# Releasing the row gathers by buffer and indices alone in a graph-convolution kernel

## The reference

```python
msg = relu(x[src] + edge_attr)                      # one message per edge
agg = segment_sum(msg, dst, num_segments=12500)
h = (1.0 + eps[0]) * x + agg
out = layernorm(x + h @ W.T + b)                    # over the 32 features
```

## Time and profile before

| what | value |
|---|---|
| time of the profiled execution | 2931.13 us |
| its span, first to last instruction | 2929.0 us (2.1 us lie around it) |
| median of the three timed runs | 2930.49 us |
| TensorE (PE) busy | 2382.3 us, 81% of the span |
| DVE / ACT / POOL busy | 1812.9 / 1635.8 / 1434.8 us (62 / 56 / 49%) |
| DMA, mean | 81 GB/s |
| mean granted clock of TensorE | 0.909 |

### The profile page before, as it was taken

The page is one execution under the profiler, slowest core; times in us unless marked ns, Lnnn a source line. Parts: engine busy times, 40 slices in busy tenths (PEclk is TensorE's granted clock), DMA queues, the critical chain, the costliest instruction groups (busy, mean ns, idle before and its releaser), DMA issues. The chain is left out here.

```text
span 2929.0 us, 110879 instructions
## 1 busy us (share of the span) xinstructions
PE 2382.3 (81%) x49112; PEld 1842.9 (63%) x35800; DVE 1812.9 (62%) x4504; ACT 1635.8 (56%) x1720; POOL 1434.8 (49%) x1467
## 2 busy tenths in 40 slices
PE   4788888888888888788888888888887878888788
PEld 2566666666666666666666666666666666666664
DVE  5766666666666666665665656666666566565665
ACT  4655555555555555555555555555555555555554
POOL 4454545544545454455455445445555545545541
PEclk9988999989989899989999999898899999898988
DMA  5333333333333333333333333333333333333332
GB/s 123 68 86 79 81 81 79 86 76 78 86 77 81 83 76 83 81 79 85 78 78 86 79 76 86 76 84 81 78 86 79 79 82 79 86 79 76 86 79 50
DMA packets 244832, 236.54 MB, mean 81 GB/s; under 512 B 107748, under 2 KB 190750, under 8 KB 244805
## 3 DMA queue, kind: packets, MB, share of 16 engines
q1 hardware_dynamic: 198053, 212.15, 31.1%
q0 software_dynamic: 46752, 24.03, 5.8%
HBM read 233.21 MB, written 2.78 MB: 81 GB/s over the span
## 5 line engine op out<-in xcount | busy, mean ns | idle before, releaser
L550 POOL DMA_INDIRECT rows_all<-in_x,index x1461 | 1434.3, 982 | 1442.6 <-PE l L1162 611.9
L1144 PE MATMUL found<-table,oh 128*128 128x128 bf16 x13312 | 1288.3, 227 | 12.7 <-issue 11.9
L1184 PE MATMUL found<-table,oh 128*128 128x128 bf16 x6656 | 1271.7, 233 | 21.2 <-issue 12.8
L1184 PEld LDWEIGHTS found<-table,oh 128*128 128x128 bf16 x6656 | 928.3, 139 | 335.8 <-issue 122.5
L1162 PE MATMUL l<-xparts,oh 128*57 128x96 bf16 x19968 | 717.0, 225 | 434.3 <-issue 434.2
L1162 PEld LDWEIGHTS l<-xparts,oh 128*57 128x57 bf16 x19968 | 590.8, 121 | 560.0 <-issue 559.2
L798 DVE COPY_PREDICATED rows_all<-mask,found 128x256 f32<-128x256 uint16 x832 | 370.3, 445 | 657.5 <-PE found L1144 507.0
L971 ACT CAST table<-l 128x768 bf16<-128x768 f32 x416 | 330.3, 795 | 661.7 <-PE l L1162 632.4
L780 DVE TENSOR_SCALAR oh<-keys,lanes 128x1024 bf16<-128x1024 f16 x624 | 295.6, 489 | 190.9 <-PE found L1144 139.8
L1015 ACT ACTIVATE oh<-keys,minus_lanes 128x1024 bf16<-128x1024 f16 x208 | 238.9, 1148 | 264.6 <-PE found L1144 222.1
L996 ACT ACTIVATE oh<-slots,minus_lanes 128x1824 bf16<-128x1824 f16 x208 | 375.2, 1804 | 6.8 <-DMA slots<-slot_dram 6.8
(11 more groups left out here) (127 smaller groups left out, 1031.0 us busy)
## 6 DMA issues: line engine op xcount, KB each, us to landing
slots<-slot_dram SPq DMA_DIRECT2D x208, 456.0 KB
keys<-key_dram SPq DMA_DIRECT2D x208, 256.0 KB
msg<-in_edge SPq DMA_DIRECT2D x208, 128.0 KB
rows_all<-in_x,index POOLq DMA_INDIRECT x1461
msg<-in_edge SPq DMA_DIRECT2D x208, 112.0 KB
index<-in_src SPq DMA_DIRECT2D x208, 3.5 KB
key_dram<-key SPq DMA_DIRECT2D x208, 2.0 KB
slot_dram<-slot_row SPq DMA_DIRECT2D x208, 3.6 KB
```

Of the source, the lines that this page charges most:

```text
L550: pool.indirect_dma_start(to, None, x, bass.IndirectOffsetOnAxis(indices[:, j:j + 1], 0)).then_inc(done, 16)
L1144: return nc.tensor.add_instruction(mybir.InstMatmult(name=nc.get_next_instruction_name(), engine=mybir.EngineType.PE, ldweights=False, ins ...
L1184: last = nc.tensor.matmul(to, key_marks(b)[:, :, t], part, start=begin, stop=end, skip_group_check=True)
```

## The change

The three turns become one. The gathers of a batch wait only until the batch that had the buffer has been added up and until the indices are there; the waits for `l1_ready` and `blocks_looked` are gone, and so are two of the three raises of `gathers_started`. The program order of everything else is as it was.

```diff
-    TURNS = [(0, 3), (3, 5), (5, POOLED)]
...
-                    for k, (j0, j1) in enumerate(TURNS):
-                        if k == 0:
-                            if not free:
-
-                                pool.wait_ge(sums_ready, b - RING + 1)
-
-                                pool.wait_ge(l1_ready, (b - RING + 2) * KEYS)
-                            pool.wait_ge(index_loaded[slot], use * 16 + 16)
-                        elif not free:
-
-                            pool.wait_ge(blocks_looked, (b - RING + 1) * KEYS + k * KEYS // 2)
-                        pool.sem_inc(gathers_started, 1)
-                        for j in range(j0, min(j1, SHORT) if isinstance(b, int) and b == 0 else j1):
-                            gather_tile(rows[slot][:, j * D:(j + 1) * D], index[slot], j, rows_gathered[slot])
+                    if not free:
+                        pool.wait_ge(sums_ready, b - RING + 1)
+                    pool.wait_ge(index_loaded[slot], use * 16 + 16)
+                    pool.sem_inc(gathers_started, 1)
+                    for j in range(SHORT if isinstance(b, int) and b == 0 else POOLED):
+                        gather_tile(rows[slot][:, j * D:(j + 1) * D], index[slot], j, rows_gathered[slot])
```

## The result

The changed kernel takes 3633.74 us (median of 4 runs, 3616.01 to 3640.16) where the kernel before takes 2929.66 us beside it: ratio 1.2394, 95% interval 1.2358 to 1.2430. The forecast was 3144 us with a range up to 3400: the sign was right, but the rise was put at 213 us and came out at 704. A row of work takes (3585.4 - 33.9) / 207 = 17.16 us where it took 13.77.

What follows compares the result with a forecast made beforehand. TensorE, busy 81%, bounds the kernel, losing 2.1 us per row to pauses from gathers. A row of 14.4 us plus 0.4 for the clock, 14.8 against 13.77, over 207 rows adds 213 to 2931: 3144 us, range 2850 to 3400.

Steps and rivals of the forecast that it cites:

- The pauses are the gathers': Bucket stage: TensorE's instructions trickle from 0.9 us after a gather's issue starts until 1.0 us after it ends.
- The rival "same": Pauses come from the loop's jump back ahead of the bucket stage, so moving gathers changes nothing: 2930 us, chance 0.07.
- The Trainium skill's rule on taken branches: A taken branch to outside the fetched window stalls; the 2.1 us would stand every loop turn, time staying 2930 us.
- Where the gathers go: Seven gathers in one 8.7 us burst, released by `add_rows`, from +4.7 to +13.4 us after the bucket stage's start.
- What comes back: Bucket stage without pauses: at most 2.1 us per row regained by TensorE.
- The pieces before: Kernel before: gathers of 3, 2 and 2, the first two pieces hidden in the table stage, the last pausing the bucket stage.
- the reserve: About 70 instructions already handed to TensorE, on which it runs at full pace before pausing; refilled between the gathers' turns.
- The trickle's price: TensorE's time per instruction while gathers hold it up: range 94 to 476 ns, 247 ns taken, giving 14.4 us per row.
- For each I follow two rows: Row lengths worked out per trickle price; at 247 ns the first row ends at 13.75 us, the second at 15.1, mean 14.4.
- the clock's 0.4: Longer starved pieces lower TensorE's granted clock: one more 1.3 us loss in three rows, 0.4 us per row.
- Faster: Rival: the burst leaves the bucket stage and the table stage carries it; 13.2 us per row, 2813 us, chance 0.22.
- Much slower: Rival: long-burst trickle with a clock drop, or rows alternating in length at 156 ns; 16.1 us per row, 3413 us, chance 0.13.

Runs made afterwards that it cites:

- experiment 8: Kernel before with its gathers in other pieces; on starved chips 4 and 3 0.9935, that a quarter early 1.0071, turns 1 and 2 a block early 1.0397.
- Experiment 4: Changed kernel with `count_ranks` moved behind the last table block: 3538.55 us, ratio 1.2346 to the kernel before, on a starved chip.

## Why the prediction had the sign and not the size

**The pauses are the gathers': right.** One gather instead of seven, or plain DMAs, takes a row from 17.16 us to about 10 on starved chips. The rival "same", that the loop's jump makes the pauses, falls with that: the jump is there in all of them. The Trainium skill's rule on taken branches ("Runtime: NRT & Kernel Launch", section Instruction fetch mechanics), weighed in the prediction, is not what stalls here: with the same jump the bucket stage's line sat idle for 16.9 us over the span with plain DMAs, where it was 158.8.

**Where the gathers go: right.** The release by `add_rows` and a run of 8.45 us (I said 8.7) stand in the timeline, and the median run starts at +4.9 (I said +4.7); no wait for the indices shows on the starved chip.

**What comes back: 1.3 us per row, where I allowed up to 2.1.** (434.3 - 158.8) / 207 = 1.33.

**The pieces before: misread.** The prediction counts two gathers in the earlier trace rows and lets the reserve fill up again between turns 1 and 2. They are the last two of a run of four, 1510.89 to 1515.96 (experiment 8). The gather of the earlier trace rows doesn't stand alone either: it is the last of four, 1016.67 to 1021.38, and shows where the effect ends, not where it begins. That it begins some 1.1 us after the first gather is seen from the late signals of the changed kernel, near the 0.9 assumed. So runs of four, whose end falls into the bucket stage, make the pauses of the kernel before, and the change joins three and four into seven.

**The trickle's price: inside the range, but taken too low.** 313 ns in the row shown and 307 as a median, where I took 247. By the prediction's own working that is worth little: its rows at 337 ns are 14.8 us, 0.4 more than its 14.4. The reserve was near: from the effect's start at 1809.5 to the first long pause at 1812.4 TensorE is not stopped and starts 68 instructions, some 59 of them reserve (an estimate: 2.9 us of trickle at 313 ns are the other 9), where I took 70.

**The step that failed is "For each I follow two rows", with 15.1 us for the second of them, and the clock's 0.4 beside it.** The first row of the pair came as forecast, 13.76 us where I had 13.75. The second took 19.9. The prediction let it begin well: a bucket stage at full clock, gathers at +4.7, and 13 instructions left for full pace when the effect ends. In the row shown the bucket stage starts at 1802.2; its last matmuls pass at half clock, the table stage starts at 1808.4 (+6.2, not +4.0), and `add_rows` ends at 1807.72, +5.5 where it was +4.6. The 4.8 us that the row took beyond 15.1 add up from three terms:

- The first gather is issued at +6.3, and the effect ends at +15.8, not +14.5: 1.3 us.
- TensorE starts again only at 1819.1, at `count_ranks`, because the signal for ACT's copy of the slots came 7.1 us late: 1.1 us.
- 42 instructions are left then, not 13, and take 3.0 us at a mean granted clock of 0.56, not 0.6 us: 2.4 us.

Two things in this were not in the sum, or too small in it. The clock was undersized: the mean granted clock fell from 0.909 to 0.811, and TensorE's busy time grew by 2572.9 - 2382.3 = 191 us, 0.92 us per row, where I gave 0.4. And late signals were not in the sum at all: I took TensorE's instructions to be late, but not its semaphores.

Over all rows, by idle time, the 3.39 us more per row are: in front of `count_ranks` (513.1 - 22.5) / 207 = +2.37, in the table stage +1.41 (325 us where it was 34), in the bucket stage -1.33, busy time +0.92; sum 3.37. The first of these I had nowhere as a place. Experiment 4 speaks against it as a cause apart: moved away, it returns as pauses.

**Faster: refuted here**, since the table stage's pauses did not stay below the 2.1 us given back: with those at `count_ranks` they are 4.1 us. **Much slower** (3413 us, 13%) was the nearest of the four. The alternation it spoke of is there, but a row of 17.16 us exceeds its 16.1, and its trickle of 156 ns is not the measured one: that it came nearest is in part luck.

**What no part of it foresaw** is the other kind of chip. There the reasoning from the trace has no object: nothing starves, and the change is a matter of 0.5%.

What stays open: what in an indexed gather holds up TensorE's instructions and signals, and what differs between the two kinds of groups, the chip or the placement. The traces show neither. That late signals and late instructions have one source is argued from their beginning and ending together, not shown. Every execution here was recorded with its span and clock, so the runs also don't tell whether recording has a part in the effect.

## What to carry to other kernels

Idle time of an engine by "issue" that keeps step with another engine's instructions can be a shared resource that the profile doesn't name: find the instruction with which it comes and goes, in a place where the usual suspects are apart, before forecasting a move of it. Waits that seem to serve no data can be pacing; before such a wait is taken out, see what joins up without it, and where that lies against the stage that uses instructions fastest. And time such a change on more than one chip and more than once: here the same edit is 24% on one and 0.5% on another.

## What the runs showed of the hardware that I had not expected

- Indexed gathers issued by POOL (0.97 us each) slow TensorE down to one instruction in 307 ns (median over 187 runs of seven gathers) and delay its signals, on some chips: ACT's copy of the slots started a median of 5.6 us after the matmul that it waits for, 7.1 us in the row shown. DVE's signal at the end of `add_rows` was not late (0.01 us). Plain DMAs of the same size and number from POOL's queue (0.58 us each) do nothing of the kind; halving the lanes of a gather takes nothing off (0.93 us each, ratio 1.2552).
- On other chips the same gathers at the same pace have no effect: the kernel before takes 2166 us there and 2865 to 2930 us here, a difference of 32 to 35%. The issuing of a gather is no faster there (985 ns, and 968 in the changed kernel on a starved chip).
- The place counts as much as the length: a run of five from the bucket stage's start costs as much (ratio 1.2399) as seven from the middle of the row (1.2371 in the same group of runs).
